# A graph network's attention rounds: query and result rows of a batch in 32 rows, the other 96 on a condition

## What is computed

```
h = relu(layernorm(x))
q = (h @ Wq + bq) * scaling ; k = h @ Wk + bk ; v = h @ Wv + bv      # 8 heads of 32
s = einsum('ehd,ehd->eh', q[row], k[col])
p = exp(s - segment_max(s, row)[row])
out = segment_sum(p / segment_sum(p, row)[row] * v[col], row)
x = x + out @ Wo + bo
h = relu(layernorm(x))
aggr = segment_sum(edge_attr, dst)
x = x + relu(relu(concat(h, aggr) @ W1 + b1) @ W2 + b2) @ W3 + b3
```

## Time and profile before

| what | value |
|---|---|
| median of 3 runs | 1770.22 us (1766.67 to 1775.79) |
| profiled execution | 1770.12 us, its span 1768.3 us |
| granted clock of PE, mean | 0.916 |
| PE busy | 1466.4 us, 83% |
| DVE busy | 1508.1 us, 85% |
| ACT busy | 925.4 us, 52% |
| POOL busy | 1017.3 us, 58%, of it 859.1 the gathers of L725 |
| DMA | 439.79 MB, queues' share of 16 engines' span 36.6% (POOL), 23.1% (SP), 14.1% (ACT) |

### The profile page before, as it was taken

The page is one execution under the profiler, slowest core; times in us unless marked ns, Lnnn a source line. Parts: engine busy times, 40 slices in busy tenths (PEclk is TensorE's granted clock), DMA queues, the critical chain, the costliest instruction groups (busy, mean ns, idle before and its releaser), DMA issues.

```text
span 1768.3 us, 26489 instructions
## 1 busy us (share of the span) xinstructions
PE 1466.4 (83%) x6685; PEld 1088.6 (62%) x6685; DVE 1508.1 (85%) x2748; ACT 925.4 (52%) x2790; POOL 1017.3 (58%) x1024
## 2 busy tenths in 40 slices
PE   4699998767888887888888888788888666899998
PEld 4545556546667666766667676666676445566664
DVE  9998887679999889998999899899999997666662
ACT  4744444466566666666656666665663111444442
POOL 6000204977777777777777777777777773422200
PEclk8699999979889999999989899999998887999999
DMA  9022526789999999999999999999999774333321
GB/s 230 9 106 102 200 101 207 234 277 335 342 328 332 328 338 335 340 340 330 336 340 334 327 344 336 339 327 343 324 332 294 230 232 144 108 112 108 107 79 39
DMA packets 237281, 439.79 MB, mean 249 GB/s; under 512 B 47022, under 2 KB 148043, under 8 KB 237121
## 3 DMA queue, kind: packets, MB, share of 16 engines
q0 software_dynamic: 72256, 216.77, 36.6%
q1 hardware_dynamic: 138408, 132.97, 23.1%
q10 hardware_dynamic: 26456, 88.28, 14.1%
HBM read 385.03 MB, written 72.44 MB: 259 GB/s over the span
## 4 chain that ended last, share of the span: by engine, by line
PE 30%; DVE 26%; issue 17%; POOL 15%; DMA 11%; ACT 1%; POOLq 0%; DVEq 0%; SPq 0%; ACTq 0%
POOL U L725 12%; DMA U<-kv_rows,dstb 9%; DVE V L1721 6%; PE bank L1388 4%; PE bank L1096 3%; DVE V L1725 3%; PE bank L1409 2%; POOL EBO L704 2%; PE bank L1097 2%; PE bank L1397 2%; DVE V L1762 2%; PE bank L1371 2%; DVE V L1456 2%; PE bank L1124 2%; PE bank L1209 2%
## 5 line engine op out<-in xcount | busy, mean ns | idle before, releaser
L725 POOL DMA_INDIRECT U<-kv_rows,dstb x856 | 859.1, 1004 | 264.7 <-issue 240.6
L1124 PE MATMUL bank<-EBO 128*128 128x256 f32 x1568 | 394.0, 394 | 18.7 <-POOL EBO L704 7.0
L1124 PEld LDWEIGHTS bank<-EBO 128*128 128x128 f32 x1568 | 303.0, 198 | 75.5 <-issue 16.3
L1209 PE MATMUL bank<-V 128*128 128x264 f32 x1136 | 314.7, 426 | 6.2 <-DVE V L1762 6.2
L1721 DVE TENSOR_TENSOR V<-U,bank_pair 128x1024 f32<-128x1024 f32 x214 | 260.3, 1216 | 60.1 <-DMA U<-kv_rows,dstb 55.7
L861 ACT ACTIVATE EBO<-EBO,ones 128x128 f32<-128x128 f32 x709 | 284.7, 402 | 23.0
L859 ACT ACTIVATE EBO<-iota,dA 128x128 f32<-128x128 f32 x709 | 279.2, 394 | 1.3 <-issue 1.1
L1209 PEld LDWEIGHTS bank<-V 128*128 128x128 f32 x1136 | 242.0, 213 | 54.9 <-DVE V L1762 7.0
L1200 PE MATMUL bank_pair<-V 128*128 128x256 f32 x256 | 92.0, 445 | 120.1 <-DVE V L1721 119.9
L1725 DVE TENSOR_REDUCE V<-V 128x32 f32<-128x1024 f32 x142 | 173.3, 1220 | 4.9
L1762 DVE TENSOR_TENSOR V<-U,bank 128x1024 f32<-128x1024 f32 x142 | 173.0, 1218 | 0.0
(11 more groups left out here) (308 smaller groups left out, 2173.5 us busy)
## 6 DMA issues: line engine op xcount, KB each, us to landing
EBO<-in_edge_attr_dram ACTq DMA_DIRECT2D x163, 512.0 KB
V<-q_rows SPq DMA_DIRECT2D x128, 128.0 KB
EBO<-in_edge_attr_dram SPq DMA_DIRECT2D x31, 512.0 KB
o_log<-R SPq DMA_DIRECT2D x108, 132.0 KB
o_log<-V SPq DMA_DIRECT2D x106, 132.0 KB
U<-kv_rows,dstb POOLq DMA_INDIRECT x856
kv_rows<-U SPq DMA_DIRECT2D x49, 256.0 KB, 2.0
ag_rows<-R SPq DMA_DIRECT2D x98, 128.0 KB
```

The lines of the kernel that those rows point to most:

```text
L725: e.indirect_dma_start(out=kvb[:, b % NKV, j, :], out_offset=None, in_=kv_dram[:, :], in_offset=bass.IndirectOffsetOnAxis(ap=dstb[:, k:k + ...
L1124: m = e.matmul(agg_bank(c)[:, 0:D], oh2[i][0:n, j, :], eb[h % NEB][0:n, j % 4, :], start=j == 0, stop=j == 7)
L1209: t = e.matmul(bank[3 + i][:, 0:RW], oho[b % NPV], PV[b % NPV][:, j, :, :].rearrange("p h d -> p (h d)"), start=j == 0, stop=j == 3)
```

## The change

A query load moves rows 0 to 31, and a second DMA moves rows 32 to 127 only if a number `wide`, worked out on DVE from the batch's first and last node, is 1. The same with the results. Since the other rows of `o_log` are then never written in most batches but are read later, they are zeroed beforehand: 27 DMAs of eight batches each on ACT's queue, one behind each projection tile from tile 22 (`ZB0`) to 48, from the same tile `low`. The `qt` buffers are zeroed once on POOL, ahead of `low`. Rows are now counted from the batch's first node, so a carry stands in row 0. Each load and each write now counts 32 on its semaphore instead of 16. SP, POOL and DVE wait for the zeros' semaphore `s_oz` before the rounds.

```diff
+        NLOW = 32
+        wide = UM.take(NW)[0:1, :].bitcast(I32)
-        CONSTS, XZ, UZ, B16, QZ, NGZ, F2Z, NID, G2Z, GZ = 11, 12, 13, 18, 21, 22, 23, 25, 26, 30
+        CONSTS, XZ, UZ, B16 = 11, 12, 13, 18
+        QZ, NGZ, F2Z, NID, G2Z, GZ = (n + NQ for n in (21, 22, 23, 25, 26, 30))
+        ZB0, ZBN = 22, 8
+        B_ZERO = 16 * ((NBT - VB + ZBN - 1) // ZBN)
...
                 r = e.value_load(nqi[0:1, b:b + 1], min_val=0, max_val=NP)
-                e.dma_start(qt[b % NQ], q_dram[bass.ds(r, P), :]).then_inc(s_q[b % NQ], 16)
+                over = e.value_load(wide[0:1, b:b + 1], min_val=0, max_val=1)
+                e.dma_start(qt[b % NQ][0:NLOW], q_dram[bass.ds(r, NLOW), :]).then_inc(s_q[b % NQ], 16)
+                e.dma_start(qt[b % NQ][NLOW:P], q_dram[bass.ds(r + NLOW, P - NLOW), :], cond=over).then_inc(s_q[b % NQ], 16)
 
             def write_rows(b):
+                over = e.value_load(wide[0:1, b:b + 1], min_val=0, max_val=1)
                 e.wait_ge(b_ev, b + 1)
-                e.dma_start(o_log[b * P:(b + 1) * P, :], R[b % NR]).then_inc(s_o[b % NR], 16)
+                e.dma_start(o_log[b * P:b * P + NLOW, :], R[b % NR][0:NLOW]).then_inc(s_o[b % NR], 16)
+                e.dma_start(o_log[b * P + NLOW:(b + 1) * P, :], R[b % NR][NLOW:P], cond=over).then_inc(s_o[b % NR], 16)
...
-            carries = o_log.rearrange("(b r) d -> b r d", r=P)[:, P - 1, :]
+            carries = o_log.rearrange("(b r) d -> b r d", r=P)[:, 0, :]
...
             e.wait_ge(lid_ready, 1)
+            e.wait_ge(hist_mm, NHC)
+            for t in qt:
+                pl.on(e.memset(t, 0.0))
             assert pl.on(e.memset(low[:, 0:RW], 0.0)) == QZ
             e.wait_ge(pl.s, QZ)
...
                 e.activation(qb[i][:, :], bq_[:, 0:D], ACT.Copy, scale=SCALE).then_inc(p_qr, 1)
+                b0 = VB + (t - ZB0) * ZBN
+                if VB <= b0 < NBT:
+                    b1 = min(b0 + ZBN, NBT)
+                    e.wait_ge(pl.s, QZ)
+                    e.dma_start(o_log[b0 * P:b1 * P, :].rearrange("(b p) d -> p b d", p=P)[NLOW:P],
+                                low[NLOW:P, 0:RW].unsqueeze(1).to_broadcast([P - NLOW, b1 - b0, RW])).then_inc(s_oz, 16)
...
-            e.tensor_copy(nqi[:, :], FL[0:1, 0, :]).then_inc(regs_ready, 1)
+            dv.on(e.tensor_tensor(wide, FL[0:1, 1, :], FL[0:1, 0, :], ALU.subtract))
+            dv.on(e.tensor_copy(nqi[:, :], FL[0:1, 0, :]))
+            e.wait_ge(dv.s, dv.n)
+            e.tensor_scalar(wide, wide, NLOW, None, ALU.is_ge).then_inc(regs_ready, 1)
             e.tensor_scalar(more[:, :], FL[0:1, 0, NBT:NBT + 1], float(NP), None, ALU.is_lt).then_inc(flags_ready, 1)
...
-            step(e.tensor_tensor(lid[:, :], node[:, :], base[:, :], ALU.subtract))
-            step(e.tensor_scalar(lneg[:, :], lid[:, :], 0.0, float(P), ALU.is_lt, ALU.mult))
-            dv.on(e.tensor_tensor(lid[:, :], lid[:, :], lneg[:, :], ALU.add))
+            dv.on(e.tensor_tensor(lid[:, :], node[:, :], fB, ALU.subtract))
```

More of the change, by code:

```diff
@@ L319, in gnn_kernel @@
         s_kvo = [sem(f"s_kvo{i}") for i in range(2)]
-        s_qz, s_fl, s_z = sem("s_qz"), sem("s_fl"), sem("s_z")
+        s_qz, s_oz, s_fl, s_z = sem("s_qz"), sem("s_oz"), sem("s_fl"), sem("s_z")
         s_eb = [sem(f"s_eb{i}") for i in range(NEB)]
@@ L438, in gnn_kernel @@
         B_IN, B_OUT, B_ALL = 16 * 5, 16 * 6, 16 * 7
+        ZB0, ZBN = 22, 8
+        B_ZERO = 16 * ((NBT - VB + ZBN - 1) // ZBN)
+        assert ZB0 + (NBT - VB + ZBN - 1) // ZBN <= NT
         def rows(w):
@@ L577, in rows_written @@
                 for i in range(NR):
-                    e.wait_ge(s_o[i], 16 * ((n + NR - 1 - i) // NR - (i < VB)))
-            carries = o_log.rearrange("(b r) d -> b r d", r=P)[:, P - 1, :]
+                    e.wait_ge(s_o[i], 32 * ((n + NR - 1 - i) // NR - (i < VB)))
+            carries = o_log.rearrange("(b r) d -> b r d", r=P)[:, 0, :]
             def load_carries(n):
@@ L586, in own_carry @@
             def own_carry(b):
-                e.dma_start(Fs[b - P:b - P + 1, 1, :], R[b % NR][P - 1:P, :]).then_inc(s_carry, 16)
+                e.dma_start(Fs[b - P:b - P + 1, 1, :], R[b % NR][0:1, :]).then_inc(s_carry, 16)
             e.wait_ge(s_qz, 48)
+            e.wait_ge(s_oz, B_ZERO)
             for i in range(2):
@@ L621, in sync_program @@
                         for i in (NBT - 6, NBT - 5):
-                            e.wait_ge(s_o[i % NR], 16 * nth(i, NR))
+                            e.wait_ge(s_o[i % NR], 32 * nth(i, NR))
                         load_carries(NBT - 4)
@@ L695, in pool_program @@
                         low[:, 0:RW].unsqueeze(1).to_broadcast([P, NB - NBT, RW])).then_inc(s_qz, 16)
-            e.wait_ge(hist_mm, NHC)
             assert pl.on(e.memset(ng[0:32, :, 0:P + 1:P], -BIG)) == NGZ
@@ L935, in write_rows @@
                 if nth(b, NR) > 1:
-                    e.wait_ge(s_o[b % NR], 16 * (nth(b, NR) - 1))
+                    e.wait_ge(s_o[b % NR], 32 * (nth(b, NR) - 1))
                 e.copy(R[b % NR], bank[3 + i][:, 0:RW]).then_inc(b_ev, 1)
@@ L1196, in q_expand @@
                 e.wait_ge(g_oh, b // SG + 1)
-                e.wait_ge(s_q[b % NQ], 16 * nth(b, NQ))
+                e.wait_ge(s_q[b % NQ], 32 * nth(b, NQ))
                 if b >= 2:
@@ L1659, in span_setup @@
                 step(e.tensor_tensor(st0[0:NH, :], cont[0:NH, :], eqFL[0:NH, :], ALU.mult))
-                step(e.tensor_tensor(eqFL[0:NH, 1:NW], base[0:NH, 0:NW - 1], base[0:NH, 1:NW], ALU.subtract))
+                step(e.tensor_tensor(eqFL[0:NH, 1:NW], FL[0:NH, 0, 0:NW - 1], FL[0:NH, 0, 1:NW], ALU.subtract))
                 step(e.tensor_scalar(eqFL[0:NH, 1:NW], eqFL[0:NH, 1:NW], float(P), None, ALU.add))
@@ L1680, in border_rows @@
                 dv.on(e.tensor_scalar(rowb[:, 1:2], pid[:, :], float(P), float(P * P), ALU.mult, ALU.add))
-                step(e.tensor_tensor(ixf[:, 0:2], nv2[:, 1, :], nv2[:, 3, :], ALU.subtract))
+                step(e.tensor_tensor(ixf[:, 0:2], nv2[:, 1, :], nv2[:, 0, :], ALU.subtract))
                 step(e.tensor_tensor(ixf[:, 0:2], ixf[:, 0:2], rowb, ALU.add))
```

## The result

| what | before | after |
|---|---|---|
| median, four runs each | 1768.57 us (1766.67 to 1775.79) | 1827.35 us (1821.72 to 1832.28) |
| profiled execution, its span | 1770.12, 1768.3 us | 1821.72, 1819.9 us |
| first gather of the rounds | 350.5 us | 395.7 us |
| from the first gather to the end of the last | 1122.1 us | 1124.2 us |
| from there to the end | 295.7 us | 300.0 us |

A forecast was written before the change was run, and what follows sets the result against it. It took POOL's pace of issuing gathers to bound the rounds and a full PE the projection. 1770.1 + 14.1 (stall) + 8 (zeros) + 2 (clock) + 0.6 (start) + 2.4 (end) - 3 (relief) = 1794 us, range 1778 to 1812.

The forecast's parts named there:

- The bound of the rounds: Rounds: they run at POOL's own pace of issuing gathers; what bytes delay is at most 6.7 us.
- rival B: Rounds: bound by bytes, 41.9 MB at 333 GB/s are 126 us, giving 1671; under 1770 had chance 0.06.
- The relief of 3 us: Rounds: fewer bytes moved save between 0 and 6.7 us, taken as 3.
- The stall: Projection, after tile 22: ACT waits for POOL's zeroed tile and PE stands still, +14.1 us.
- The zeros: Projection: 27 zero DMAs of 2.15 to 2.3 us beside each tile's writes, 3.3 of 3.72 us, barely fit.
- +8: Projection: us added because ACT is held at its zero DMAs until POOL's zeros end near 207; between 0 and 12.
- The sentence on pending DMAs: ACT's queue: about three DMAs pending, then the issuer stands; held from the fourth zero DMA for 11 us.
- The clock: PE: time lost to a lower clock after two stops, partly hidden in waits, +2 us (0 to 4).
- The end: Last four batches' writes: SP's added steps delay the border gathers, +2.4 us (0.4 to 3.0).
- SP in the rounds: Rounds: SP's added register loads and conditional DMAs make 4.6 of 5.24 us per batch; nobody waits.
- rival C: Rounds: SP becomes the bound, lengthening them by 34 us to 1828; with longer blocking, over 1806, chance 0.13.
- The changed profile: Expected trace: ACT idle 17 us, transposes at 188, first gather near 375, gathers unchanged, DMA share in rounds about 0.86.

The follow-up runs named there:

- spread_always: spread, but the 96 rows of queries and results move in every batch, without the condition; 1776.51 us, ratio 1.004.
- late27: The kernel after, but the zeros go on ACT's queue from tile 27 on, ten batches per DMA; 1820.52 us, ratio 1.028.
- spread: The kernel after, but POOL's zeros and 80 batches early on POOL's queue, 134 batches on SP's queue behind tiles 2 to 46; 1777.13 us.
- late27_big: late27, but each zero DMA writes three rows a packet from 32 partitions, same bytes; 1824.03 us, ratio 1.031.
- pool_zeros: The kernel after, but the 27 zero DMAs stand on POOL's queue behind its own zeros, no wait or DMA on ACT; 1828.68 us.
- half_stall: half_nostall, but ACT's zeros from tile 22 on, four batches each, with ACT's wait for POOL's zero tile; 1799.38 us, ratio 1.016.
- spread_end: spread, but SP writes the last four batches' 128 result rows with one plain DMA, without register load and conditional DMA; 1772.28 us.
- half_nostall: The kernel after, but half the zeros early on POOL's queue, half on ACT's from tile 27, five batches each, no stall; 1781.04 us.

## Why the prediction was right and wrong

**The bound of the rounds** was right. The gathers kept 998 ns and their pace; 41.9 MB less bought nothing, and rival B fell, by the kernel after and by spread_always. The relief of 3 us was not there: from the first gather to the end of the last the twelve kernels with the change's rounds take 1123.5 to 1126.3 us, the two without it 1122.1 and 1122.9. The sum was off by 5 us here. What makes the train some 2 us longer was not isolated; it is not the bytes, since spread_always has 1125.6.

**The stall** was right in place and length: 17.23 us of ACT, 13.7 of PE forecast as 14.1, ready at 187.0 and found at 187.77. Wrong was that it adds. It is worth 18.3 us where DMA has room, and 6.8 (by the medians of the kernel after and late27; 8.2 with the kernel before beside each) where the stretch is bound by bytes: while PE stood, the zeros and POOL's own drained, so tiles behind it were less late. What is left of it may be bytes again: 27 tiles stand beside the zeros in the kernel after and 22 in late27, and five tiles are 2 MB, at 270 GB/s an estimated 7 us.

**The zeros** are the step that failed: "Sum 3.3 of 3.72 us: it fits, barely". Two things in it were wrong. First the rate. I priced a zero DMA at 2.15 to 2.3 us, by the rate of the projection's own writes and by that of the rounds, 333 GB/s, which are mostly gathers; a packet of it was to hold an engine for 0.046 us and held it for 0.060. The stretch in fact moved 266 to 273 GB/s at a share of 0.92 to 0.93: 0.81 + 0.39 MB per tile are 4.4 us, not 3.3. None of the full stretches read in the kernel before has this rate: its own large writes ran at 353 to 358 GB/s. Second, the balance was drawn per tile and not over the stretch. 21.7 + 4.2 MB of zeros and 27 tiles of 0.39 are 36.5 MB; even at 333 GB/s that is 110 us, while PE's 27 tiles take 100. A total over the stretch would have shown that POOL's 4.2 MB find no room to be made up in, and that the cost does not end near 207 us, as "+8" assumed, but at the last zero. By 333 GB/s it would have warned of 10 us, not of the 44 below. At 270 GB/s it is 135 us, from 187 to 322; the last zero DMA was issued at 313.6. Term by term, 8 us stood for what late27 against spread measures as 44 (50.5 and 6.5 us over the kernel before beside each).

The sentence on pending DMAs was right as a mechanism. ACT was to be held from its fourth zero DMA, for 11 us, until POOL's dump ends near 207; it was held at its sixth, for 5.7 us from 212.8 on, and the dump landed at 218.6. But it does not set the pace: where it is gone, in late27_big and, up to 260 us, in pool_zeros, the tiles wait for SP's writes instead and are as late.

The Trainium skill, DMA: Bandwidth & Descriptors, section "Specifications", puts the limit of HBM for a core near 358 GB/s, and by that figure the 36.5 MB are an estimated 102 us. The stretch shows 273 GB/s at a share of 0.93, and the measurement decides: that limit is no price for these transfers. The kernel before did come to 358 GB/s, in the 5 us from 200 with POOL's own zeros in them. I had used the section to argue over the rounds, where it did not bind, and not over the projection, where bytes did.

**The clock**: +2 us was for two short stops. The stop of 13.7 us costs 5.2 by the windows of half_stall, 3.5 of it right behind it and 1.7 behind a second, short stop. In the kernel after it is drowned in the bytes.

**The end**: +2.4 forecast, 4.3 measured, and spread_end gets 3.5 of it back. The size of a step was off. In SP's timeline the four writes and their carry rows of after:

```profile
1537.94 0.33 SPq L544 DMA_DIRECT2D o_log<-V  x1
1538.55 0.08 SPq L545 DMA_DIRECT2D o_log<-V  x1
1538.67 0.91 SPq L597 DMA_DIRECT2D EBO<-V  x1
1540.67 0.35 SPq L544 DMA_DIRECT2D o_log<-V  x1
...
1546.79 0.33 SPq L544 DMA_DIRECT2D o_log<-R  x1
1547.80 0.33 SPq L545 DMA_DIRECT2D o_log<-R  x1
1548.18 0.82 SPq L597 DMA_DIRECT2D EBO<-R  x1
```

From the first write to the second are 2.73 us, where 1.74 stood before and 2.25 was forecast; from the first write to the last carry row 10.24, where the earlier trace rows gives 5.68. The conditional DMA that moves nothing costs 0.08 us, not 0.37. But it starts 0.28 us after the DMA ahead of it has been issued (0.68 in the last batch, where it moves its rows), and that gap had no term.

**SP in the rounds** was right: its waits for results fell from 593 to 169 us between 400 and 1450 us, forecast to some 150 in all; rival C fell. Its time, 1828, is the measured one by chance: the rounds lengthened by 2 us, not by 34. **The changed profile**: ACT's 17 us, the transposes at 188 and the gathers' pace were as described, and the third turn came at 201.84 instead of near 199. The zero DMAs issued faster than the "over 2 us, one for about 10" (1.24 in the median, 5.7 at most); the first gather at 395.7 instead of 375 was the number that said at once which part was wrong. DMA's share in the rounds fell to 0.90, not 0.86.

No version here beats the kernel before. The best with the change, spread_end, stands at 1.0011 (1.0001 to 1.0021). Whether the zeroing could be left out was not tried.

## What to carry to other kernels

Before putting transfers beside busy work, add up all bytes of the whole stretch, those already there too, and divide by a rate read from like traffic; if that comes near the stretch's length, nothing fits, and a stall in the same stretch is no longer a separate price. Like traffic has to be alike in more than its direction: the large writes of the kernel before ran at 353 GB/s, the stretch with the new ones at 273, and only a run shows that. The same 21.7 MB cost 44 us in 22 tiles and nothing over 45 tiles and an idle beginning. And look first whether the bytes saved were what the saved stretch waited for.

## What the runs showed of the hardware

- With DMA full or nearly so, zeros from 96 partitions beside the tiles' writes ran at 257 to 284 GB/s (windows of 25 us and more at a share of 0.92 or over), zeros from 128 partitions beside the same writes at 353 to 358, mostly gathers at 333 to 337. Packets of 3 KB from 32 partitions gave no more than those of 1 KB from 96 (250 and 270 GB/s). What makes the difference was not separated.
- In spread the zeros from 96 partitions and the tiles' writes took a share of 0.58 for 189 GB/s; in the full stretch of the kernel after a share of 0.93 for 273. Per share that is 326 against 294 GB/s.
- A conditional DMA that moves nothing took SP 0.08 us, and one that moves 0.33.
- ACT issued zero DMAs in 0.32 us each while they landed in 5.7 us (median), and in 1.24, at most 5.7, when they landed in 10.8. The time to landing is not what blocks: late27_big's, 320 packets each, landed in 17.9 and issued in 0.32, and half_nostall's, 480 rows each, in 0.32 too, while late27's, 960 rows each, landed in 14.4 and took 3.0.
- A stop of 13.7 us and the one of 1.9 us behind it cost PE 5.2 us of clock beside the stop.
